# Scatters of a routed kernel made to wait for TensorE's steps and for the pages' silus

## What is computed

```
x = x + conv_block(layer_norm_over_channels(x))
t = tokens(x)                                   # 16384 tokens of 64 numbers
n = layer_norm(t)
logits = n @ gate_w + gate_b                    # 16 experts, the best two are kept
dispatch = one_hot(top 2) * (their probabilities, made to sum to 1)
hidden = silu(n @ w1[e]) * (n @ w2[e])          # 64 -> 128, for an expert e
t = t + sum over e of dispatch[e] * (hidden @ w3[e])
```

## Time and profile before

| | before |
|---|---|
| median of three runs | 655.66 us (653.53 to 656.78) |
| the profiled execution | 656.09 us |
| its span, first to last instruction | 654.3 us |
| mean granted clock of PE over the span | 0.844 |
| PE, DVE, ACT, POOL busy | 77%, 67%, 60%, 44% |
| scatters of the first stage (L468) | 128, from 83.6 to 325.3 us |
| result scatters (L484) | 147, from 335.1 us on |

### The profile page before, as it was taken

One profiled execution on the slowest core, in us unless ns is written; L12 is line 12 of the kernel. 1 busy time (PEld: TensorE's weight loads), 2 busy tenths in 40 slices (PEclk: granted clock), 3 DMA queues, 4 the chain that ended last, 5 costly groups with the idle time before them and its releaser, 6 DMA issues.

```text
span 654.3 us, 14180 instructions
## 1 busy us (share of the span) xinstructions
PE 506.6 (77%) x4186; PEld 439.2 (67%) x4186; DVE 440.3 (67%) x1242; ACT 394.6 (60%) x946; POOL 287.2 (44%) x378
## 2 busy tenths in 40 slices
PE   5899967647391955205399999999999999989964
PEld 5576645535270644105289999999999999979964
DVE  4666755436272858806088888888888888868853
ACT  4766854434361642005088888888878788858850
POOL 3000062725445265772625555455444444535452
PEclk8877896859595865557679999999999999989986
DMA  7911110010100000112122222222324143420133
GB/s 280 278 48 33 34 55 15 25 45 20 49 14 23 11 29 14 44 42 58 46 50 53 51 53 49 42 52 57 79 48 115 42 116 80 114 43 15 47 106 128
DMA packets 62664, 40.97 MB, mean 63 GB/s; under 512 B 50004, under 2 KB 54319, under 8 KB 62081
## 3 DMA queue, kind: packets, MB, share of 16 engines
q1 hardware_dynamic: 52208, 23.84, 16.0%
q0 software_dynamic: 8800, 8.94, 4.1%
q10 hardware_dynamic: 1584, 7.29, 2.9%
HBM read 21.46 MB, written 19.19 MB: 62 GB/s over the span
## 4 chain that ended last, share of the span: by engine, by line
PE 45%; DVE 15%; another core or an unknown queue 13%; issue 12%; ACT 11%; DMA 1%; ACTq 0%; POOL 0%; SPq 0%; DVEq 0%; POOLq 0%
PE up L936 8%; PE up L938 7%; PE up L768 6%; PE turn L952 4%; PE lines L969 4%; PE small L784 3%; DVE hidden L1553 2%; ACT xc L668 2%; DVE xs_lo L1478 2%; DVE hidden L1558 2%; PE up L743 2%; PE lines L971 2%; PE small L917 2%; PE turn L796 2%
## 5 line engine op out<-in xcount | busy, mean ns | idle before, releaser
L484 POOL DMA_INDIRECT results<-result,page_in x147 | 153.8, 1046 | 164.6 <-ACT xc L668 96.1
L468 POOL DMA_INDIRECT pages<-payload,slot_int x128 | 127.3, 995 | 184.8 <-DVE slot_int L1379 147.0
L936 PE MATMUL up<-up_w,xs_hi 128*128 x588 | 162.7, 308 | 27.0 <-DVE xs_lo L1478 22.1
L938 PE MATMUL up<-up_w,xs_lo 128*128 x588 | 149.3, 286 | 6.0 <-issue 6.0
L936 PEld LDWEIGHTS up<-up_w,xs_hi 128*128 128x128 f32 x588 | 113.4, 193 | 32.3 <-issue 29.4
L668 ACT ACTIVATE xc<-up 128x512 f32<-128x512 f32 x147 | 89.4, 608 | 72.0 <-PE up L938 53.7
L938 PEld LDWEIGHTS up<-up_w,xs_lo 128*128 128x128 f32 x588 | 114.1, 194 | 5.4 <-issue 5.4
L1553 DVE SCALAR_TENSOR_TENSOR hidden<-up,page_in,xc 128x128 f32<-128x128 f32 x196 | 59.2, 342 | 29.5 <-ACT xc L668 23.7
L1563 DVE TENSOR_TENSOR hidden_lo<-turn,hidden_hi 128x512 f16<-128x512 f32 x98 | 66.7, 681 | 1.4 <-ACT hidden_hi L681 1.2
L952 PE MATMUL turn<-ident,hidden 128*128 128x128 f32 x392 | 60.5, 277 | 5.5 <-DVE branch L1563 4.3
L681 ACT ACTIVATE hidden_hi<-turn 128x512 f16<-128x512 f32 x98 | 61.3, 626 | 0.6 <-PE turn L952 0.6
(11 more groups left out here) (262 smaller groups left out, 1037.1 us busy)
## 6 DMA issues: line engine op xcount, KB each, us to landing
pages<-up_w ACTq DMA_DIRECT2D x4, 1332.0 KB, 10.6
page_in<-pages SPq DMA_DIRECT2D x147, 36.0 KB
page_in<-pages SPq DMA_DIRECT2D x147, 32.0 KB
x_in<-in_x SPq DMA_DIRECT2D x7, 512.0 KB
out<-up_raw SPq DMA_DIRECT2D x5, 512.0 KB
results<-result,page_in POOLq DMA_INDIRECT x147
up_raw<-in_L_ffn_w SPq DMA_DIRECT2D x4, 512.0 KB, 17.2
pages<-payload,slot_int POOLq DMA_INDIRECT x128
```

Of the source, the lines that this page charges most:

```text
L468: pool.indirect_dma_start(out=pages, out_offset=bass.IndirectOffsetOnAxis(ap=slot_int[q % PAYLOADS][:, t:t + 1], axis=0), in_=payload[q % ...
L484: pool.indirect_dma_start(out=results, out_offset=bass.IndirectOffsetOnAxis(ap=page_in[g % LOADS][:, k, D + AT_TOKEN:D + AT_TOKEN + 1].bit ...
L936: pe.matmul(target, xs_hi[g % 2][:, k * P:(k + 1) * P], weights[:, bass.ds(e * 2, 2 * HID)], start=True, stop=False)
L938: last = pe.matmul(target, xs_lo[g % 2][:, k * P:(k + 1) * P], weights[:, bass.ds(e * 2, 2 * HID)], start=False, stop=True)
```

## The change

`scatter` gets a call ahead of each of its 16 DMAs. It makes POOL wait, for tile 4, until the gate product of the pair two behind is there; for tiles 7, 10 and 13 until PE has turned the choice, made the counts and made the ranks of the next pair; for tile 8 of the last but one pair until the first group of pages is turned; and the 16 of the last pair go by the silus of pages 0 to 11 (tile 0 and 1 after one silu, tile 15 after twelve). Nothing else is touched.

```
 def let_through(q, t):
     if t == 4 and q + 2 < PAIRS:
         pool.wait_ge(gate_ready, q + 3)
     if t == 7 and q + 1 < PAIRS:
         pool.wait_ge(chosen_turned, q + 2)
     if t == 10 and q + 1 < PAIRS:
         pool.wait_ge(counts_ready, q + 2)
     if t == 13 and q + 1 < PAIRS:
         pool.wait_ge(ranks_ready, q + 2)
     if t == 8 and q == PAIRS - 2:
         pool.wait_ge(rows_turned, 1)
     if q == PAIRS - 1:
         pool.wait_ge(silu_done, 1 + 3 * t // 4)

 def scatter(q):
     ...
     for t in range(TILES):
+        let_through(q, t)
         pool.indirect_dma_start(
```

More of the change, by code:

```diff
@@ L461, in _ @@
             pool.wait_ge(blanked, 64)
+            def let_through(q, t):
[9 more added lines that the diff above has]
+                    pool.wait_ge(rows_turned, 1)
+                if q == PAIRS - 1:
+                    pool.wait_ge(silu_done, 1 + 3 * t // 4)
             def scatter(q):
```

## The result

| | before | after |
|---|---|---|
| median | 654.6 us (653.08 to 656.78, 4 runs) | 603.94 us (602.71 to 607.48, 4 runs) |
| ratio, with its 95% interval | | 0.923 (0.918 to 0.928) |
| span of the profiled execution | 654.3 us | 601.4 us |
| PE's granted clock over the span | 0.844 | 0.892 |

The change makes the kernel 51 us faster.

What follows compares the result with a forecast made beforehand. Unbroken POOL scatters were taken to delay news of PE's finished work, leaving some 60 us of first-stage waiting. 656.1 - 26 (rounds) - 4 (pair 4) - 10 (stage change) - 5 (first pages) = 611 us; forecast range 598 to 628, eight-in-ten 586 to 645.

Steps and rivals of the forecast that it cites:

- Rounds of pairs 0 to 4: First stage: breaks let PE's updates out earlier, 26 us less in pairs 0 to 3 and 4 us less in pair 4.
- I take 28.5 us a round: Rounds of pairs 0 to 3: predicted length with the breaks, bounds 24 and 33 us; four rounds fall from 139.9 to 114.
- rival A: Whole kernel: breaks let everything out, rounds 24 to 25 us, first pages lose nothing; 582 to 598 us; chance 0.20.
- Change of stages: Pair 6's scatters: POOL stops at tile 7's end, first pages rounded at 287.8 us instead of 297.92; 10 us less.
- First pages: Rounding to silu 12: 39.6 us instead of 44.6, so 5 us less (16 less to 4 more).
- the good pace: Page stage: one scatter every 2.12 us, at which nothing is held up; the bad pace is 1.26.
- the result scatters start some four pages later ... so this is hidden: First pages: the page load waiting for them is needed at page 29, some 30 us later, so no cost.
- B: Only the stages' change helps: rounds stay 33 us, gain 8 + 10 us, 630 to 645 us; chance 0.15.
- D: Slower: each break costs its drain and frees no step; rounds 2.8 us longer, 677 us in all; chance 0.07.
- C: Nothing changes: late updates have another cause and only coincide with the scatters; 656 us; chance 0.08.
- the rule of the Trainium skill: Whole kernel: a DMA never contends with a compute engine, so scatters could not slow PE; the gain would be zero.
- all five late reads that end with the last scatter: Rounds and page start: cited against the no-effect rival, together with rounds of 21.10 against 35.58 us.

Runs made afterwards that it cites:

- whole_change: The changed kernel as it is, timed on chip 8 beside the kernel before: 609.81 us against 652.06, ratio 0.937.
- rounds_again: Kernel before plus only the waits at tiles 4, 7, 10 and 13, on chip 2: 611.61 us, ratio 0.932.
- silus_again: Kernel before plus only the pacing of the last pair's 16 scatters by silus, on chip 4: 543.24 us, ratio 1.002.
- timed_breaks: Kernel before plus about 3 us of POOL memsets ahead of tiles 7 and 13 of pairs 0 to 4, no waits for PE, chip 2: 622.58 us, ratio 0.952.
- turn_again: Kernel before plus only pair 6's tile 8 wait for the first turned pages, on chip 2: 653.73 us, ratio 0.995.
- small_rows: Kernel before with scatters writing 16 bytes of each row into a separate tensor, results zero-filled early, on chip 4: 550.28 us, ratio 1.016.
- few_rows: Kernel before with scatters writing 16 rows of 128, results zero-filled early, on chip 4: 551.56 us, ratio 1.016.

## Why the prediction was right, and where not

The time, 603.94 us, lies in the forecast's own range (598 to 628 us), 7 us below its value of 611. The mechanism was right where the updates are late: breaks let them out. That the value came so close is in part chance. The rounds gave 10.2 us more than predicted and the change of stages 1.2, the first pages 9.1 less, and 5.7 came from stretches that the sum put at nothing: 8 us in all, and the profiled execution took 603.12 us. The terms:

- **Rounds of pairs 0 to 4**, 30 us less predicted (26 and 4), 40.2 measured (36.0 and 4.2). The step that was off is "I take 28.5 us a round": pairs 2 and 3 take 24.6, which is the undisturbed end of my own bounds. Up to the logarithm the working held (11 us predicted, 11.65 measured; the drain 1.5 us, not 2.4). What I added behind it, 1 to 2 us for tiles 13 to 15 on top of the next round's start and a stop for the counts, is not in the trace: tile 10 does not wait, tile 13 waits 1.62 us beside DVE's and PE's own work. Only the first two rounds, 28.07 and 26.73 us, are near what I had put for all four. In pairs 2 and 3 rival A's rounds are what came. What decides is whether POOL stops at tile 7. Of the twelve rounds of pairs 0 to 3 in after, whole_change and rounds_again the four where it does take 24.6 to 24.7 us, the eight where the choice is out in time 26.4 to 28.1. The prediction has it stop in every round.
- **Change of stages**, 10 us predicted, 11.2 measured (46.3 to 35.1). The prediction counts one wait in pair 6, where the change puts four (tiles 7, 8, 10 and 13). The ranks' wait at tile 13 alone is worth 4.0 us (rounds_again); here the turn's wait comes first. PE turns the pages, POOL stops, the rounding comes 2.7 us after the end of the scatter ahead (244.02 - 2.93 = 241.09 us), and POOL goes on beside it:

```profile
234.83 1.12 PE L933 MATMUL small<-ident,page_in 128*128 128x128 f32 x4 [1.16 <-DMA page_in<-pages]
```

```profile
244.02 0.95 POOL L484 DMA_INDIRECT pages<-payload,slot_int  x1 [2.93 <-remote]
```

```profile
243.77 0.60 ACT L677 ACTIVATE xs_hi<-small 128x512 fp32r<-128x512 f32 x1 [14.11 <-remote]
```

- **First pages**, 5 us less predicted. To silu 12 it is 2.3 less (44.6 to 42.3), but to silu 16 it is 4.1 more. Silu 2 comes 16.0 us after the rounding, as predicted (16.2). From there to silu 12 it is 26.3 us, 5.1 over the good pace, where I had put 2: this term was mis-sized. From silu 12 to 16 it is 14.6 us in place of 8.2, and there the step that failed is "the result scatters start some four pages later ... so this is hidden". I looked only at who waits for the results, not at what they do to PE's updates. They are queued behind the last scatter, which now waits for twelve silus (page 11's), are mostly due by then, and so come in a train at 1.30 us; the next silu stands for 4.73 us, until the fifth of them, started at 291.62 us, is nearly through. POOL, then ACT:

```profile
285.17 0.96 POOL L484 DMA_INDIRECT pages<-payload,slot_int  x1 [1.02 <-ACT xc L684]
286.44 1.00 POOL L500 DMA_INDIRECT results<-result,page_in  x1 [0.30 <-issue]
...
291.62 0.98 POOL L500 DMA_INDIRECT results<-result,page_in  x1 [0.30 <-issue]
```

```profile
286.03 0.63 ACT L684 ACTIVATE xc<-up 128x512 f32<-128x512 f32 x1
...
292.40 0.60 ACT L684 ACTIVATE xc<-up 128x512 f32<-128x512 f32 x1 [4.73 <-remote]
```

  On the quick chip the same train runs (result scatters 1.3 us apart from 251.0 us on in silus_again, over ten of them) and no silu is late.
- **Not forecast:** 2.8 us less ahead of the first scatter, where the change does nothing and whole_change and rounds_again have 84 to 85 us: no gain of the change. And 2.9 us less from silu 16 to the end. The runs with the turn's wait have 299.2 to 301.1 us there, those without it 303.3 to 303.6 (chip 4 left out), so it goes with that part; why is open.

The sum of the table is 654.3 - 2.8 - 40.2 - 11.2 + 4.1 - 2.9 = 601.4 us, up to rounding.

Of the rivals, B is wrong (the rounds gain 40 us, not 8), D too (rounds with two stops are 8 to 12 us shorter than without, outside pair 0's). A was right on the rounds of pairs 2 and 3 and wrong on the first pages. C, the only one that rested on the rule of the Trainium skill, is refuted on chip 2 by timed_breaks. What is late there is the news of finished work and not the work: PE is busy for 21.24 us in turn_again's round of pair 3 and for 20.68 in rounds_again's. On chip 4, where no part of the change is worth anything, C's outcome is the one that came (the whole change was not run there). That a chip could decide between them was in none of my cases.

One argument against C was too strong. Of its "all five late reads that end with the last scatter" four do. The turned choice of rows 5 is read at 163.99 us, 8.2 us before the last scatter of that train ends. So an update can come out in a train as well, only late.

## What to carry to other kernels

When several engines' waits end 1.5 to 4 us after the last of a train of POOL's DMAs, and the steps that they wait for ended long before, a short break in the train, best tied to the step whose update is wanted, can be worth 8% of the kernel without any work taken out. Put it just behind the step that the longest chain hangs on, and see in the trace that POOL does stop there: in whole_change it did not, and the rounds were up to 3 us longer. Then ask what is queued behind the break, as it comes out as a train of its own: the turn's wait alone gained 10.9 us and lost 11.4 in this way. And time such a change on more than one chip before you believe its gain, for here its main part is worth 7% on one chip and nothing on another.

## What the runs showed of the hardware

The same kernel takes 652 to 655 us on chips 2, 8 and where it was first timed, and 542 us on chip 4. There is no profile of the kernel before from chip 4; silus_again stands for it, as its time is the same there (ratio 1.002). The difference, 654.3 - 541.0 = 113.3 us, lies in the rounds (64.0), the change of stages (24.5), the first pages (16.6) and the rest (8.5), by the table above. On chip 4 POOL's train goes on over several rounds with hardly a break (the rows below are from silus_again: pair 3's round, the change of stages and the first pages, then scatter 0 of pair 3 on POOL, the turned choice and the logarithm on ACT) and nothing is late: the choice is read 3.0 us and the logarithm 4.7 us after scatter 0, against 12.2 and 22.87. (POOL starts a pair's scatters later in PE's round there, so the missing waits say more than these times.)

```profile
146.60:167.10 20.50, 19.13 (x125) 14.10 (x125) 17.39 (x58) 15.79 (x39) 15.62 (x17) 0.92 0.09 30
...
187.90:209.68 21.78, 8.49 (x47) 5.44 (x47) 19.71 (x62) 2.10 (x6) 17.21 (x16) 0.50 0.20 49
209.68:245.91 36.23, 32.42 (x306) 31.19 (x307) 31.64 (x98) 28.47 (x71) 27.38 (x30) 0.93 0.37 80
```

```profile
146.56 0.96 POOL L474 DMA_INDIRECT pages<-payload,slot_int  x1 [0.30 <-issue]
```

```profile
149.54 0.38 ACT L602 ACTIVATE chosen_t<-lines 128x256 bf16<-128x256 bf16 x1 [0.28 <-PE lines L828]
...
151.28 0.27 ACT L538 ACTIVATE log_var<-small,both_eps 128x16 f32<-128x16 f32 x1
```

Scatters have the same length, 0.96 us, and the same pace, 1.26 us, on both kinds of chip. One more thing differs in the traces: on the other chips they miss records of the updates by which DMAs tell that they have landed. Each scatter raises its semaphore by 16, which makes 2048 updates for the 128 scatters. The packed traces hold 446 of them in before, 641 in after and 432 to 628 in the runs on chips 2 and 8, but 2013 to 2046 in the seven runs on chip 4 that have scatters. So the list of DMA issues has a time to landing for the scatters of silus_again, its last number, and none for those of after:

```profile
pages<-payload,slot_int POOLq DMA_INDIRECT x128, 2.2
```

```profile
pages<-payload,slot_int POOLq DMA_INDIRECT x128
```

It is the same with SP's loads of the input and its stores of the output (3.4 and 3.6 us in silus_again, none in after). PE's updates have records too. The one for the turned choice of rows 5 is dated 20 ns ahead of ACT's reading at 163.99 us. So it is the update that comes late, and not ACT that is slow to see it. All this fits a path for updates, or for their records, that is full or slow on those chips. That is argued, not shown.

Nor is a train of scatters enough by itself to make an update late, even on such a chip. Before, POOL starts scatters from 251.62 to 294.06 us with no gap above 0.31 us between them, and yet pair 7's choice, turned at 271.64 us, reaches ACT at once; the first pages, turned by 278.20 us in the same train, are late by 20 us.

```profile
272.07 0.38 ACT L596 ACTIVATE chosen_t<-lines 128x256 bf16<-128x256 bf16 x1 [14.54 <-issue]
```

Two of this train's scatters were slow ones, at 257.99 and 260.27 us; whether that, or how much the other engines do meanwhile, decides, no run tells.

Three things more are open. The first is whether it is the chip at all: chip 4 was quick both times, chips 2 and 8 were tried once each, and what else ran beside the kernel is not on record. The second is the profiler: every time here, before's too, comes with a span and a clock from a record of the execution, and the chips with the late updates are those whose traces lack records, so whether updates are late when nothing is recorded was not tested. The third is whether the bytes, the descriptors or the starts of the scatters hold the updates back; small_rows and few_rows would tell on a chip of the slow kind.
